# The order of a spectral stage, and how its correlation is formed: a decoder layer on one core

## The reference

```python
qf = jnp.fft.fft(q, axis=2)
kf = jnp.fft.fft(k, axis=2)
corr = jnp.fft.ifft(qf * jnp.conj(kf), axis=2).real
w, idx = jax.lax.top_k(corr.transpose(0, 1, 3, 2), 8)
w = jax.nn.softmax(w, axis=-1)
pos = jnp.arange(L)[:, None]
for i in range(8):
    g = jnp.minimum(idx[:, :, None, :, i] + pos, L - 1)
    out = out + w[:, :, None, :, i] * jnp.take_along_axis(v, g, axis=2)
...
out = jnp.einsum('bser,eor->bso', route_weight[..., None] * h, Bw)
```

## Time and profile before

| | |
|---|---|
| median of 3 runs | 868.9 us (867.91 to 870.41) |
| the profiled execution | 867.83 us, span of the trace 866.0 us |
| TensorE busy | 792.1 us, 91% of the span |
| VectorE busy | 589.9 us, 68% |
| ACT busy | 412.6 us, 48% |
| GpSimd busy | 242.5 us, 28% |
| mean granted clock of TensorE | 0.986 |

### The profile page before, as it was taken

One profiled execution on the slowest core, in us unless ns is written; L12 is line 12 of the kernel. 1 busy time (PEld: TensorE's weight loads), 2 busy tenths in 40 slices (PEclk: granted clock), 3 DMA queues, 4 the chain that ended last, 5 costly groups with the idle time before them and its releaser, 6 DMA issues. The chain is left out here.

```text
span 866.0 us, 10640 instructions
## 1 busy us (share of the span) xinstructions
PE 792.1 (91%) x3512; PEld 561.5 (65%) x3512; DVE 589.9 (68%) x1291; ACT 412.6 (48%) x647; POOL 242.5 (28%) x196
## 2 busy tenths in 40 slices
PE   3889999999999999999999999999778888888875
PEld 1336778878888888888888888877534444444432
DVE  5988855478984775665676476244658787878773
ACT  7884664456652643553453544112134445454531
POOL 0001221224444333432433333121123223232321
PEclk9999999999999999999999999999999999999997
DMA  7373110023230131131122020200000101010100
GB/s 216 117 244 133 62 37 1 1 85 98 71 107 32 55 105 37 37 113 46 37 78 81 14 72 13 72 0 13 0 13 25 45 29 50 26 50 25 49 14 37
DMA packets 25655, 50.57 MB, mean 58 GB/s; under 512 B 3264, under 2 KB 3648, under 8 KB 25600
## 3 DMA queue, kind: packets, MB, share of 16 engines
q1 hardware_dynamic: 25600, 49.89, 17.8%
HBM read 45.68 MB, written 4.19 MB: 58 GB/s over the span
## 5 line engine op out<-in xcount | busy, mean ns | idle before, releaser
L673 PE MATMUL ps<-x_hi,w_hi 128*128 128x512 f32 x448 | 176.1, 393 | 0.1
L675 PE MATMUL ps<-x_hi,w_lo 128*128 128x512 f32 x448 | 174.7, 390 | 0.0
L674 PE MATMUL ps<-x_lo,w_hi 128*128 128x512 f32 x448 | 174.4, 389 | 0.0
L789 POOL TENSOR_TENSOR h_lo<-hf,h_hi 128x512 fp32r<-128x512 f32 x56 | 73.9, 1320 | 243.3 <-ACT h_hi L784 243.2
L798 DVE TENSOR_TENSOR acc<-acc,ps 128x512 f32<-128x512 f32 x112 | 76.4, 685 | 75.7 <-PE ps L675 75.7
L673 PEld LDWEIGHTS ps<-x_hi,w_hi 128*128 128x128 f32 x448 | 84.1, 188 | 20.8 <-issue 3.3
L777 DVE TENSOR_TENSOR hf<-hf,ps 128x512 f32<-128x512 f32 x56 | 38.5, 687 | 85.6 <-PE ps L675 85.6
L675 PEld LDWEIGHTS ps<-x_hi,w_lo 128*128 128x128 f32 x448 | 84.1, 188 | 18.0
L674 PEld LDWEIGHTS ps<-x_lo,w_hi 128*128 128x128 f32 x448 | 84.2, 188 | 17.3
L530 POOL TENSOR_TENSOR w_lo<-wt,w_hi 128x512 fp32r<-128x512 f32 x42 | 62.3, 1484 | 113.9 <-ACT w_hi L523 113.9
L673 PE MATMUL ps<-w_hi,h_hi 128*128 128x512 f32 x224 | 88.5, 395 | 5.6 <-DVE acc L798 4.2
(11 more groups left out here) (151 smaller groups left out, 1396.7 us busy)
## 6 DMA issues: line engine op xcount, KB each, us to landing
codes_sb<-in_codes SPq DMA_DIRECT2D x40, 256.0 KB, 3.0
scale_sb<-in_scale_rows SPq DMA_DIRECT2D x80, 128.0 KB, 2.9
lft<-in_lora_ft SPq DMA_DIRECT2D x14, 512.0 KB, 4.3
acc<-in_x SPq DMA_DIRECT2D x4, 1024.0 KB, 8.2
ctx<-in_ctx SPq DMA_DIRECT2D x16, 256.0 KB, 2.6
out<-fin SPq DMA_DIRECT2D x16, 256.0 KB, 2.1
codes_sb<-in_codes SPq DMA_DIRECT2D x5, 512.0 KB, 3.4
codes_odd<-in_codes SPq DMA_DIRECT2D x4, 512.0 KB, 5.3
```

Source lines behind the costliest of these rows:

```text
L673: nc.tensor.matmul(bank, hi, rhs_hi, start=start, stop=False)
L674: nc.tensor.matmul(bank, hi, rhs_lo, start=False, stop=False)
L675: return nc.tensor.matmul(bank, lo, rhs_hi, start=False, stop=stop)
L789: nc.gpsimd.tensor_tensor(h_lo[:, c % 2, i], hf[:, i], h_hi[:, c % 2, i].bitcast(F32), ALU.subtract).then_inc(hlo_done, 1)
```

## The change

- corr is formed in two steps. **inverse** (`pe_inverse`): the inverse matrix is held and the spectra `pp` move, two matmuls of 64 columns as in gather. ACT copies the result to `by_lag` (`act_inverse`), and corr is now four transposes of it.
- The order of a slot on every engine is another, and route, its turn and copy, and expert belong to tile v-3, gather and x3 to tile v-2. Four tiles are under way at a time.
- TensorE: turn_h (v-3), kc (v), gather 0 (v-2), q (v), gather 1 (v-2), kn, inverse (v), route (v-3), lags (v-1), corr (v), negacyclic (v-1), turn of wh (v-3), cyclic (v-1), expert (v-3).
- VectorE: mark (v-1), product (v), x3 (v-2), weigh (v-1), stats (v-2), the routing steps (v-3), rstd (v-2), top (v), its subtraction into topd, cyclic (v-1), final (v-3), sum (v), and **less** (v), the subtraction into cd, which was part of top before.
- ACT: the copy of kc (v), the exponential of cd (v-1), the copies of kn and inverse (v), of lags (v-1), of wh (v-3), x3's normalising (v-2), the copy wns (v-1), the exponential of topd (v), the copy of turn_h (v-2), the normalising of xq (v+2).
- GpSimd: en (v-1), the power (v-2), pn (v-1).
- The statistics of the third chunk move from ahead of the stage into slot 1 and those of the fourth into slot 5 (`LATER`), behind x3 on VectorE, each with its power on GpSimd in the same slot and its root (`x_rstd`) in the next.
- Ahead of the stage the first two tiles' steps are spread among the last down projections. On SyncE the loads of tiles 0 and 1 are issued ahead of the slots, and the store of a tile is two slots later.
- lags, turn_h and inverse share bank 1, gather and expert bank 4. rw's operand `sc` is in PSUM (bank 5) rather than in SBUF.

The diff, cut; the orders of the other engines' slots are as listed above.

```diff
+    by_lag = two("by_lag", at=h_at + 2 * 2 * CH * 4)
...
-    CORR, LAGS, QW, MISC, ROUTE, KW = 0, 1, 2, 4, 5, 6
+    CORR, MISC, QW, GATHER, ROUTE, KW = 0, 1, 2, 4, 5, 6
...
     def pe_kn(pe, t, b):
+        pe.wait_ge(ctx_in_s[b], 16 * (t // 2) + 16)
         pe.wait_ge(kc_copied, t + 1)
...
+    def pe_inverse(pe, t, b):
+        pe.wait_ge(prod, t + 1)
+        if t == 0:
+            pe.wait_ge(hmul_done, 2 * NG * NCH - 1)
+        elif t == 1:
+            pe.wait_ge(lag_copied, 1)
+        elif t == 2:
+            pe.wait_ge(inverse_copied, 2)
+        else:
+            pe.wait_ge(h_copied, t - 2)
+        for s in range(2):
+            mm = nc.tensor.matmul(ps[s * L:(s + 1) * L, MISC], spec[:, INV, 0:L], pp[:, b, s],
+                                  start=True, stop=True)
+        mm.then_inc(inversed, 1)
+
+    def act_inverse(act, t, b):
+        act.wait_ge(inversed, t + 1)
+        if real(t - 1):
+            act.wait_ge(corr_ready, t - 1)
+        else:
+            act.wait_ge(down, SUB * (NCH * NG - 1))
+        nc.scalar.copy(by_lag[:, b], ps[:, MISC]).then_inc(inverse_copied, 1)
+
     def pe_corr(pe, t, b):
-        pe.wait_ge(prod, t + 1)
+        pe.wait_ge(inverse_copied, t + 1)
         if real(t):
             pe.wait_ge(marked, t)
             pe.wait_ge(less_done, t)
         else:
             pe.wait_ge(hmul_done, 2 * NG * NCH - 1)
         for j in range(KT):
-            for s in range(2):
-                mm = nc.tensor.matmul(ps[:, CORR, j * P + s * L:j * P + (s + 1) * L],
-                                      pp[:, b, s, j * P:(j + 1) * P], spec[:, INV, 0:L],
-                                      start=True, stop=True)
+            ch = slice(j * P, (j + 1) * P)
+            mm = nc.tensor.transpose(ps[:, CORR, ch], by_lag[:, b, ch], eye[:])
         mm.then_inc(corr_ready, 1)
...
         pe.wait_ge(weighed, t + 1)
         if t == 0:
-            pe.wait_ge(added, 4 * NCH * NG)
-        if real(t):
-            pe.wait_ge(x3_done, t)
+            pe.wait_ge(inverse_copied, 1)
+        elif t == 15:
+            pe.wait_ge(h_copied, 14)
+        else:
+            pe.wait_ge(inverse_copied, t + 2)
         for j in range(KT):
             ch = slice(j * P, (j + 1) * P)
-            mm = nc.tensor.transpose(ps[:, LAGS, ch], wl[:, b, ch], eye[:])
+            mm = nc.tensor.transpose(ps[:, MISC, ch], wl[:, b, ch], eye[:])
         mm.then_inc(lag_turned, 1)
     def pe_cyclic(pe, t, b):
         pe.wait_ge(lag_copied, t + 1)
-        pe.wait_ge(prod, min(t + 2, TT))
-        if real(t):
-            pe.wait_ge(pcyc, t)
+        if t == 15:
+            pe.wait_ge(pcyc, 15)
+        else:
+            pe.wait_ge(prod, t + 2)
         by_sequence(pe, QW, SPEC, wts[:, b]).then_inc(wc_ready, 1)
     def pe_negacyclic(pe, t, b):
         pe.wait_ge(lag_copied, t + 1)
-        pe.wait_ge(kn_copied, min(t + 2, TT))
-        if real(t):
-            pe.wait_ge(wn_copied, t)
+        if t == 15:
+            pe.wait_ge(wn_copied, 15)
+        else:
+            pe.wait_ge(kn_copied, t + 2)
...
     def pe_gather(pe, t, b, k):
         if k == 0:
-            pe.wait_ge(lag_copied, t + 1)
             pe.wait_ge(pcyc, t + 1)
+            if t == 0:
+                pe.wait_ge(added, 4 * NCH * NG)
+            if t == 0:
+                pass
+            elif t == 1:
+                pe.wait_ge(x3_done, 1)
+            else:
+                pe.wait_ge(fin_done, t - 1)
         else:
             pe.wait_ge(pneg, 2 * t + 2)
         mat, src = ((OUT, pc), (OUT_N, pn))[k]
         for s in range(2):
-            mm = nc.tensor.matmul(ps[s * L:(s + 1) * L, LAGS], spec[:, mat, 0:L], src[:, b, s],
+            mm = nc.tensor.matmul(ps[s * L:(s + 1) * L, GATHER], spec[:, mat, 0:L], src[:, b, s],
                                   start=(k == 0), stop=(k == 1))
...
     def pe_turn_h(pe, t, b):
         pe.wait_ge(xh3_done, t + 1)
-        if real(t):
-            pe.wait_ge(fin_done, t)
+        if t == 15:
+            pe.wait_ge(h_copied, 15)
+        else:
+            pe.wait_ge(lag_copied, t + 2)
...
         logits = ps[:, ROUTE, P:P + E]
+        sc = ps[:, ROUTE, 3 * P:3 * P + E]
...
     def pe_expert(pe, t, b):
         pe.wait_ge(wh_copied, t + 1)
-        pe.wait_ge(h_copied, t + 1)
-        nc.tensor.matmul(ps[:, MISC], wht[:, b], eb[:], start=True, stop=True).then_inc(expert, 1)
+        if t == 15:
+            pe.wait_ge(fin_done, 15)
+        else:
+            pe.wait_ge(x3_done, t + 2)
+        nc.tensor.matmul(ps[:, GATHER], wht[:, b], eb[:], start=True, stop=True).then_inc(expert, 1)
...
+    LATER = (1, 5)
...
-                    if g == NG - 1 and c >= 1:
-                        if c >= 2:
-                            x_rstd(dve, NCH + c - 2)
+                    if g == NG - 1 and c >= 2:
+                        x_rstd(dve, NCH + c - 2)
+                    if g == NG - 1 and 1 <= c < 3:
                         x_stats(dve, NCH + c - 1)
             dve_top(dve, 0, 0)
+            dve_top_less(dve, 0, 0)
+            dve_less(dve, 0, 0)
+            dve_mark(dve, 0, 0)
+            dve_sum(dve, 0, 0)
             dve_add(dve, NG - 1, NCH - 1, 0)
             dve_add(dve, NG - 1, NCH - 1, 1)
-            dve_sum(dve, 0, 0)
-            dve_mark(dve, 0, 0)
+            dve_weigh(dve, 0, 0)
             dve_add(dve, NG - 1, NCH - 1, 2)
             dve_add(dve, NG - 1, NCH - 1, 3)
-            x_rstd(dve, NCH + 2)
-            x_stats(dve, NCH + 3)
-            x_rstd(dve, NCH + 3)
...
-                        pe_corr(pe, 0, 0)
+                        pe_inverse(pe, 0, 0)
                     pe_down(pe, *last, 3)
-            for s in range(SUB):
-                pe_down(pe, NG - 1, 0, NCH - 1, s)
+            pe_corr(pe, 0, 0)
+            pe_kc(pe, 1, 1, 0)
+            pe_down(pe, NG - 1, 0, NCH - 1, 0)
+            pe_kn(pe, 1, 1)
+            pe_down(pe, NG - 1, 0, NCH - 1, 1)
+            pe_q(pe, 1, 1)
+            pe_down(pe, NG - 1, 0, NCH - 1, 2)
+            pe_lags(pe, 0, 0)
+            pe_down(pe, NG - 1, 0, NCH - 1, 3)
```

More of the change, by code:

```diff
@@ L213, in build @@
     x3t = two("x3t")
-    mx, sc, m2, rw = two("mx", (8,)), two("sc", (E,)), two("m2", (8,)), two("rw", (E,))
+    mx, m2, rw = two("mx", (8,)), two("m2", (8,)), two("rw", (E,))
     wh, wht = two("wh", (P,)), two("wht", (P,))
@@ L903, in pe_q @@
             pe.wait_ge(hmul_done, 2 * NG * NCH)
-        else:
+        elif t > 1:
             pe.wait_ge(pcyc, t - 1)
@@ L971, in dve_top, with dve_top_less, dve_less @@
         mm.then_inc(top_done, 1)
-        largest = top[:, b, :, 0:1]
+    def dve_top_less(dve, t, b):
         dve.wait_ge(top_done, t + 1)
-        nc.vector.tensor_tensor(topd[:, b], top[:, b], largest.to_broadcast([P, 8, TOPK]),
+        nc.vector.tensor_tensor(topd[:, b], top[:, b], top[:, b, :, 0:1].to_broadcast([P, 8, TOPK]),
                                 ALU.subtract).then_inc(topd_done, 1)
-        nc.vector.tensor_tensor(rows(cd, b), corr, largest.to_broadcast([P, 8, L]),
+    def dve_less(dve, t, b):
+        corr = ps[:, CORR].rearrange("p (r l) -> p r l", l=L)
+        dve.wait_ge(top_done, t + 1)
+        if real(t - 1):
+            dve.wait_ge(exp_done, t - 1)
+        nc.vector.tensor_tensor(rows(cd, b), corr, top[:, b, :, 0:1].to_broadcast([P, 8, L]),
                                 ALU.subtract).then_inc(less_done, 1)
@@ L1052, in act_lags @@
             act.wait_ge(wn_ready, t - 1)
-        nc.scalar.copy(wts[:, b], ps[:, LAGS]).then_inc(lag_copied, 1)
+        nc.scalar.copy(wts[:, b], ps[:, MISC]).then_inc(lag_copied, 1)
     def act_negacyclic(act, t, b):
@@ L1113, in pe_route @@
         if real(t):
+            pe.wait_ge(wh_done, t)
             pe.wait_ge(wh_copied, t)
@@ L1169, in sp_store, with slots, at @@
         sp.dma_start(row_of(out, t), fin[:, b]).then_inc(out_s[b], 16)
-    DEEP = 3
-    def slots(e, piece, first=1):
-        for v in range(first, TT + DEEP):
-            def at(stage):
+    def slots(e, piece, deep):
+        for v in range(TT + deep):
+            def at(stage, first=0):
                 t = v - stage
-                return (t, t % 2, t // 2) if 0 <= t < TT else None
+                return (t, t % 2, t // 2) if first <= t < TT else None
             piece(at)
     LEAD = ATT + PER
+    LATER = (1, 5)
     with nc.Block() as block:
@@ L1228, in _ @@
                 sp.dma_start(dst[:], src).then_inc(const_in, 16)
+            for t in range(2):
+                sp_ctx(sp, t, t)
             def piece(at):
-                if a := at(0):
-                    sp_ctx(sp, a[0], a[1])
-                if a := at(3):
-                    sp_store(sp, a[0], a[1])
-            slots(sp, piece, 0)
+                if a := at(0, 2):
+                    sp_ctx(sp, *a[:2])
+                if a := at(5):
+                    sp_store(sp, *a[:2])
+            slots(sp, piece, 5)
             for b in range(2):
@@ L1292, in _ @@
```

(16 more changed lines are left out.)

148 lines of the change are left out of this document (82 added, 66 removed).

## The result

The changed kernel takes 834.3 us as the median of four runs (833.93 to 834.81), the kernel before 868.4 (867.91 to 870.41): a ratio of 0.960 with an interval of 0.959 to 0.962. The profiled execution took 834.53 us with a span of 832.7. The forecast was 834.

What follows compares the result with a forecast made beforehand. Bound before: a loop of TensorE and VectorE waiting for each other. Sum: 643.0 + 12 x 12.4 + 2.3 + 35 = 829.1, plus 4.3 and 1.1, gives 834.5, say 834 us; range 823 to 850.

Steps and rivals of the forecast that it cites:

- The bound of before: Spectral stage before: a loop of TensorE and VectorE waiting for each other, no engine at its limit, period 14.14 us.
- TensorE laid end to end: TensorE's new order in one period: its steps, every change of shape paid, sum to 12.4 us, 0.2 of it standing.
- Rival 1: TensorE's changes of shape are free or half price; VectorE's loop then holds the period at 11.7: 825 us, chance 0.17.
- Rival 3: Direct changes between row and column halves on TensorE cost far more than 0.2; at 0.8 each 876 us, chance 0.05.
- The correlation's method, -0.46: TensorE, per period: old corr's 1.93 us removed, inverse 1.02 and four transposes 0.45 added, net -0.46.
- Each need in time: Waits of one period on all engines: needs covered, except 0.2 ahead of negacyclic; VectorE has next to no slack.
- Rival 2: A wait replaces the removed ones, each 0.5 us late adding 0.5 to the period; with two, 849 us, chance 0.18.
- a limit of 11.7: VectorE's loop of product, inverse, route and 7.8 us of VectorE would hold the period at about 11.7 us.
- rw at nothing on the path: rw's operand in PSUM gives VectorE 0.67 us, hidden by TensorE's 12.4; with the lock back, up to +0.5 a period.
- The join: Gated network into spectral stage: product(2) at 632.1 us, product(3) at 643.0, against 657.86 before.
- Slot 5, +2.3: Second moved statistics in slot 5: 3.0 us and 0.6 for the root, less about 1.3 of waits filled, +2.3.
- The end, 35: From product(15) to the end of the last final: 35 us, bounds 32 and 38, against 36.1 before.

Runs made afterwards that it cites:

- the kernel with the light gather: Changed kernel without gather 0's matmuls and with gather 1 moving only the first 128 of its 512 columns: 824.2 us in one run, period 11.34.
- the old order with rw free: Kernel before with only rw's operand sc moved to PSUM, plus the wait its bank needs: 861.0 us, ratio 0.9899, period 13.49.
- the three kernels that leave work out: Changed kernel without gather 0's matmuls: 824.2 us; also without one of gather 1's two matmuls: 821.4; instead with gather 1 moving 128 of 512 columns: 824.2.

## Why the prediction was right, point by point

**The bound of before.** Right that it was a loop through both engines and not an engine at its limit. The runs show what was in it: rw held by en, 0.65 of the 14.14 (rw's operand in PSUM, old order). topd held by pn was another 0.33, which the prediction gave 0 to 0.3; it is on that loop, as the old order with the new method lost 0.42 and gained 0.33 of it back when topd fell to 0.22.

**TensorE laid end to end.** Right: 12.38 against 12.4, with 0.24 of waiting ahead of negacyclic against 0.2. The doubtful term was the direct change between row halves and column halves, taken at 0.2. It is 1.06 and 1.01 a step in the rows, and two changes less are worth 0.35. Rivals 1 and 3 fall with it: free changes would have shown q at 0.86, and 0.7 us each would have shown 1.56. One step was mispriced: expert, behind cyclic now and so behind a change of shape, was laid out at 0.9 and takes 1.06. Route at 1.12 instead of 1.19 and 0.01 to 0.02 less in nearly every other step made up for it. The page TensorEngine Tiling (Array Packing) of the Trainium skill, section Tiling Modes, says that changing the mode drains the engine, and the rows agree so far as a change costs 0.15 to 0.20 us; that it is a drain they do not show.

**The correlation's method, -0.46.** This step failed in its meaning though the sum holds. The durations were right (1.01 for inverse, 0.43 for corr), but the removed 1.93 was the price behind negacyclic, a change of shape included, and in the new order the same work costs 1.73. I priced what is removed from its old place and what is added in its new one. With the wait for wts that the longer corr hides, the method gives 0.02 less than nothing in a period. Its real worth is 4.7 us once in the whole kernel, most of which the rows show in slot 5, and I had not seen it.

**Each need in time.** Right for kc, product, inverse, lags and gather 1: no bracket ahead of any of them. Rival 2 fell: the slack of VectorE is 1.40 us, not "next to no". By the kernel with the light gather the next loop needs 11.34, so it is 1.04 shorter than the period. I had overstated VectorE's own work by 0.3 and so named a limit of 11.7, and for a loop that is not the next one. It didn't touch the sum, because TensorE was above both. Rival 1's 825 us was too high by some 4, an estimate: with free changes TensorE's own 11.4 of my sum would have held, and 0.3 of period is 14 x 0.3 us.

**rw at nothing on the path.** Right, and for a stronger reason than given: with the operand back in SBUF the time is the same. The warning of "up to +0.5 a period" was wrong, since it took rw to stay beside en in the new order, where rw starts 4.2 us after en has ended.

**The join.** product(2) came at 633.13 (632.1 said), product(3) at 643.80 (643.0). product(1) was 0.5 early (622.20), but the stretch to product(2) took 10.93 and not 9.4, because TensorE stood 1.91 us for product(1) and then ran at the lower level for a while:

```profile
623.48 1.08 PE L959 MATMUL ps<-pp,spec 128*64 128x512 f32 x4 [1.91 <-DVE pp L946]
625.24 1.11 PE L981 MATMUL ps<-eye,by_lag 128*128 128x128 f32 x4 [0.69 <-ACT by_lag L969]
626.28 3.14 PE L890 MATMUL ps<-wts,spec 64*128 64x512 f32 x8
```

In the repeat of the same kernel TensorE stood the same 1.91 us, but the clock stayed up (negacyclic and cyclic took 1.99 instead of 3.14), and product(1) to product(2) was 9.32 us instead of 10.93; my sum of 9.4 was that case, though its terms, added up as they stand in the prediction, give 9.1 with VectorE's 10.9 and 9.4 only with 11.2.

**Slot 5, +2.3.** Measured +1.44. Only the wait that lags gets (1.22) and little else comes through; VectorE's slack took more of the 3.6 than I allowed.

**The end, 35.** Measured 36.4, within the bounds. The last three tiles run with long waits, and TensorE then at the lower level (route 2.18 for 1.19, expert 2.07 for 1.12 in the last one), which I had not laid out; the kernel before has the same rows there. With the statistics back ahead of the stage TensorE had the same waits there (1.96 and 1.33 us), but route still took 1.19, and the end took 34.0. So the 35 lies between the two cases and is no better known than that.

The total is closer (834.3 against 834) than its parts deserve, and that is luck: join +0.8 and end +1.4 were offset in part by slot 5, -0.9, and twelve periods of 0.02. The 1.1 that remained for the end of the last final (830.17 against 829.1) was offset by the 1.1 that the sum added for the median over the profiled execution, where now the median is 0.2 below it.

**Still open.** Why product(0) comes up to 3.5 us earlier or later from run to run in the same kernel; it moves the total by more than some of the terms. Nor was it tried why the clock fell in the join and at the end in one execution and not in another with the same waits. How the 1.1 of period between the old order with rw free (13.49) and the new one (12.38) divides among its moves was not taken apart; topd is 0.33 at most of it.

## What to carry to other kernels

When no engine is full, look for the loop that runs through two of them, and for instructions in it that are longer than their twins elsewhere; one operand moved out of SBUF was worth 0.65 of 14.14 us here without any reordering. Once one engine's queue is gap-free, its order is still a cost: put matmuls of one shape together. Price work that is taken out by what it would cost in its new place, beside its new neighbours, not by what it cost in the old.

## What the runs showed of the hardware

- Into a step of two 64-row halves or of two 64-column halves a change of shape costs TensorE 0.15 to 0.21 us, from the other kind of halves as from full width (1.06 or 1.07 against 0.86, 1.01 or 1.02 against 0.86).
- Two 64-column matmuls of 512 columns in float32 take 1.01 us together and one alone takes the same.
- A wait of 1.22 us in slot 5 left TensorE's clock at its upper level; one of 2.22 in the same place was followed by the lower level for some 7 us, and matmuls of 1.90 and 1.13 us took 3.26 and 2.08. In the three kernels that leave work out the wait there was 1.89 us, and negacyclic then took 1.75 to 2.08 instead of 1.13. In the join a wait of 1.91 us was followed by the lower level in one execution of the changed kernel and not in the other.
- Two small VectorE steps with both inputs in SBUF ended within 0.1 us of the GpSimd step beside them: topd took 0.55 instead of 0.22, rw 0.89 instead of 0.23. With one of its inputs in PSUM rw took 0.23 in the middle of the same GpSimd step.
